# Bias rows in four row tiles, and the output gate's constants moved from POOL to PE for four of six quads

## What is computed

```
x = x + triangle_attention(_gn(x))        # 4 heads of 32, one softmax row of 96 per (i, q, head)
x = x + triangle_multiplication(_gn(x))
```

```
a = mask * sigmoid(zn @ a_g_w.T + a_g_b) * (zn @ a_p_w.T + a_p_b)
b = mask * sigmoid(zn @ b_g_w.T + b_g_b) * (zn @ b_p_w.T + b_p_b)
t = einsum('ikh,jkh->ijh', a, b)
gate = sigmoid(zn @ g_w.T + g_b)
out = gate * (layernorm(t; ln_out_w, ln_out_b) @ z_w.T + z_b)
```

## Time and profile before

| | us |
|---|---|
| runs | 279.98, 281.68, 281.94 |
| median | 281.68 |
| profiled execution, its own time | 281.32 |
| span of its profile | 279.4 |
| busy: PE, DVE, ACT, POOL | 237.3, 210.9, 208.3, 144.1 |

### The profile page before, as it was taken

The page is one execution under the profiler, slowest core; times in us unless marked ns, Lnnn a source line. Parts: engine busy times, 40 slices in busy tenths (PEclk is TensorE's granted clock), DMA queues, the critical chain, the costliest instruction groups (busy, mean ns, idle before and its releaser), DMA issues.

```text
span 279.4 us, 7233 instructions
## 1 busy us (share of the span) xinstructions
PE 237.3 (85%) x2580; PEld 195.4 (70%) x2580; DVE 210.9 (75%) x368; ACT 208.3 (75%) x953; POOL 144.1 (52%) x132
## 2 busy tenths in 40 slices
PE   7569793769999989999999999999979999587930
PEld 7459530757788878788877878888758866386930
DVE  4025892437999989999999989998755849959790
ACT  0374744369999989999999999999846755569490
POOL 1620000008777667777677777675600029998082
PEclk9957959598999999999999999999999999965695
DMA  9300013653444464436453554440000000000028
GB/s 153 50 3 2 1 28 102 205 191 132 159 167 166 167 216 159 159 134 207 164 202 116 174 175 167 149 147 2 2 2 0 0 2 4 0 4 0 0 42 129
DMA packets 42455, 27.12 MB, mean 97 GB/s; under 512 B 24468, under 2 KB 42420, under 8 KB 42420
## 3 DMA queue, kind: packets, MB, share of 16 engines
q1 hardware_dynamic: 31564, 25.22, 27.6%
q10 hardware_dynamic: 10856, 1.45, 3.3%
HBM read 1.36 MB, written 1.18 MB: 9 GB/s over the span
## 4 chain that ended last, share of the span: by engine, by line
PE 41%; ACT 17%; DVE 13%; SPq 8%; issue 7%; ACTq 5%; DMA 5%; POOL 2%; POOLq 1%; DVEq 0%
ACT maps L667 11%; PE psum L1197 5%; SPq L434 5%; DMA u_st<-u_split 5%; PE psum L1074 4%; PE psum L1161 3%; PE psum L1006 3%; PE psum L1208 3%; PE psum L1164 2%; PE psum L1162 2%; PE psum L1139 2%; PE psum L1096 2%; PE psum L1267 2%; DVE shared L987 2%; SPq L413 2%
## 5 line engine op out<-in xcount | busy, mean ns | idle before, releaser
L667 ACT ACTIVATE maps<-psum,neg_max 96x96 f32<-96x96 f32 x384 | 123.6, 353 | 7.8 <-DVE neg_max L925 5.8
L493 POOL TENSOR_TENSOR maps<-maps,rden 96x768 f32<-96x768 f32 x48 | 70.4, 1467 | 79.2 <-DVE rden L935 72.8
L667 ACT ACTIVATION_READ_ACCUMULATOR maps<-psum,neg_max 96x1 f32 x384 | 83.9, 220 | 0.0
L941 DVE COPY turned<-psum 96x1024 f32<-96x1024 f32 x48 | 58.5, 1219 | 8.0 <-PE psum L1197 7.9
L925 DVE TENSOR_REDUCE neg_max<-psum 96x8 f32<-96x768 f32 x48 | 45.8, 954 | 8.8 <-PE psum L1164 8.5
L1197 PE MATMUL psum<-ident,maps 96*96 96x96 f32 x384 | 40.1, 247 | 0.0
L1161 PE MATMUL psum<-u_st,x_stack 128*96 128x384 f32 x96 | 36.6, 382 | 3.3 <-ACT maps L667 2.2
L1162 PE MATMUL psum<-bias_hi,ident_r 128*96 128x384 f32 x96 | 32.8, 341 | 0.0
L1164 PE MATMUL psum<-bias_lo,ident_r 128*96 128x384 f32 x96 | 32.7, 341 | 0.0
L1197 PEld LDWEIGHTS psum<-ident,maps 96*96 96x96 f32 x384 | 32.1, 126 | 0.0
L1208 PE MATMUL psum<-turned 128*32 128x96 f32 x768 | 25.8, 252 | 0.8 <-DVE turned L941 0.8
(11 more groups left out here) (179 smaller groups left out, 423.7 us busy)
## 6 DMA issues: line engine op xcount, KB each, us to landing
u_st<-u_split SPq DMA_DIRECT2D x96, 192.0 KB
x_stack<-shared SPq DMA_DIRECT2D x40, 96.0 KB, 2.0
maps<-in_x ACTq DMA_DIRECT2D x4, 144.0 KB, 4.6
maps<-in_x SPq DMA_DIRECT2D x4, 144.0 KB, 4.0
x_stack<-shared SPq DMA_DIRECT2D x4, 144.0 KB, 2.1
out_y<-maps SPq DMA_DIRECT2D x6, 96.0 KB, 3.1
out_y<-maps ACTq DMA_DIRECT2D x6, 96.0 KB, 3.4
bias_lo<-gate_sb SPq DMA_DIRECT2D x24, 12.0 KB
```

Source lines behind the costliest of these rows:

```text
L493: pool.tensor_tensor(at, at, rden[:, rows, :].unsqueeze(3).to_broadcast([N, 2, H, N]), ALU.mult).then_inc(probs_ready, 1)
L667: e = act.activation(probs[:, k % SLOTS, n, h], bank_s[r % 4][0:N, h * N:(h + 1) * N], ACT.Exp, bias=neg_max[:, r % BODY, h:h + 1], accum_ ...
L941: dve.tensor_copy(turned[0:N, j % 2].rearrange("p r x -> p (r x)"), psum[0:N, 2 * BANK:4 * BANK]).then_inc(t_ready, 1)
```

## The change

**Bias rows.** Rows 0 and 1 of `tri_b` are copied by three DMAs of SP's queue to rows 32, 64 and 96 (and the ones of `ones_r` are set there by three more memsets of DVE at the start). The bias matmul of member f then uses the 32 partitions of f alone.

**Constants.** For quads 2 to 5, gate * constant is no longer added to the residual by POOL. The gate of these quads is multiplied by 1/root before it meets the product, so PE puts constant * root into the bank first and adds the product to it: gate/root * (root * constant + z) = gate * (constant + z/root). For that the root `tok[:, 2]` (now stored in the order of blocks) is transposed by PE, copied by ACT to `deviation_t`, and multiplied by PE with `const_rows`, 96 partitions x 1024, in which POOL has spread `z_const` over the blocks with a 0/1 matrix `selected`. POOL adds gate * constant for the first 8 blocks alone (3 steps in place of 8).

The new tiles lie in memory that attention has left by then, and the reciprocal root is read in the order of blocks:

```
-        gate_const = u_split[0:N, 0:2].bitcast(f32).rearrange("j s t n -> j s (t n)")[:, :, 0:GROUP * HD].rearrange(
-            "j s (b f c) -> j s b f c", f=GROUP, c=C)
+        late = u_split.bitcast(f32).rearrange("p s t n -> p (s t n)")[0:N]
+        const_rows = late[:, 0:2 * 4 * HD].rearrange("p (e x) -> p e x", e=2)
+        deviation_t = late[:, 2 * 4 * HD:2 * 4 * HD + N]
+        selected = late[:, 2 * 4 * HD + N:2 * 4 * HD + N + C]
+        gate_const = late[:, 3 * GN:5 * GN].rearrange("j (s b f c) -> j s b f c", s=2, f=GROUP, c=C)
...
+        CONST_SETS = -(-4 * POOL_QUADS // TRIO)
...
-        inverse = tok[:, 3].rearrange("j b f -> j (b f)").rearrange("j (f b) -> j b f", f=GROUP)
+        inverse = tok[:, 3]
```

SP, behind the last `stage(g)`; PE waits for it before the last idle products of attention (`pe.wait_ge(rows_copied, 16 * (GROUP - 1))`):

```
+            sp.wait_ge(rows_split, 1)
+            for f in range(1, GROUP):
+                sp.dma_start(tri_b[f * C:f * C + 2, :].bitcast(f32), tri_b[0:2, :].bitcast(f32)).then_inc(rows_copied, 16)
```

POOL, behind its last `step_pool`:

```
             pool.wait_ge(z_prep_copied, 1)
-            for n in range(SETS):
-                product = gate_const[:, n % 2, 0:TRIO]
+            pool.wait_ge(selection_made, 1)
+            pool.tensor_tensor(const_rows.rearrange("p e (m c) -> p (e m) c", c=C),
+                               selected.unsqueeze(2).to_broadcast([N, C, C]),
+                               z_const[:, None, 0:C].to_broadcast([N, C, C]), ALU.mult).then_inc(const_spread, 1)
+            for n in range(CONST_SETS):
+                at = slice(TRIO * n, min(TRIO * n + TRIO, 4 * POOL_QUADS))
+                blocks = at.stop - at.start
+                product = gate_const[:, n % 2, 0:blocks]
                 pool.wait_ge(gates_ready, 2 * n + 2)
...
```

ACT, behind the six copies of the tail:

```
             act.wait_ge(var_ready, 5)
-            act.activation(tok[:, 2], tok[:, 1], ACT.Sqrt).then_inc(root_ready, 1)
+            act.activation(tok[:, 2], tok[:, 1].rearrange("j b f -> j (b f)").rearrange("j (f b) -> j b f", f=GROUP),
+                           ACT.Sqrt).then_inc(root_ready, 1)
+            act.wait_ge(deviation_turned, 1)
+            act.activation(deviation_t, banks[0][0:N, 0:N], ACT.Copy).then_inc(deviation_copied, 1)
```

DVE, at its start, at the end of `z_preparation`, and behind `gate_z(1)`:

```
+            for f in range(1, GROUP):
+                dve.memset(ones_r[f * C:f * C + 2, :].bitcast(f32), 1.0)
...
+                dve.tensor_reduce(selected, ident[0:N, 0:N].rearrange("p (g m) -> p m g", m=C), AX.X,
+                                  ALU.add).then_inc(selection_made, 1)
...
-            dve.wait_ge(const_gated, 2 * QUADS)
```

PE, in `project(n)` (the bias matmul of `z_const` in `norm_front(1)` is cut to 32 partitions in the same way):

```
                 for f in range(GROUP):
-                    pe.matmul(projection_bank(n, f)[0:N, 0:TRIO * PW], ones_r[:, :],
-                              tri_b[:, None, 0:PW].to_broadcast([P, TRIO, PW]), start=True, stop=False)
+                    rows = slice(f * C, (f + 1) * C)
+                    pe.matmul(projection_bank(n, f)[0:N, 0:TRIO * PW], ones_r[rows, :],
+                              tri_b[rows, None, 0:PW].to_broadcast([C, TRIO, PW]), start=True, stop=False)
```

PE, in the tail, where the six quads' transposes now stand in a loop of their own ahead of this:

```
+            def z_constant(q):
+
+                rows = slice(32 * (q // 2), 32 * (q // 2) + 32)
+                pe.matmul(z_bank(q)[0:N, :], deviation_t[rows, :], const_rows[rows, q % 2, :], start=True, stop=False)
...
+            z_products(0)
+            pe.wait_ge(tn_ready, QUADS)
+            pe.wait_ge(root_ready, 5)
+            pe.transpose(banks[0][0:N, 0:N], tok[:, 2].rearrange("j b f -> j (b f)"), ident[0:N, 0:N]).then_inc(deviation_turned, 1)
+            z_products(1)
+            pe.wait_ge(deviation_copied, 1)
+            pe.wait_ge(const_spread, 1)
+            for n in range(2):
+                for q in range(POOL_QUADS + n, QUADS, 2):
+                    z_constant(q)
+            for q in range(POOL_QUADS, QUADS):
+                z_products(q)
```

More of the change, by code:

```diff
@@ L336, in res_bank @@
             return 4 + q % RES_BANKS
-        Z_AFTER = 5
         W_ALL = 3 * HD + H + 6 + C
@@ L508, in _ @@
             pool.wait_ge(z_prep_copied, 1)
-            for n in range(SETS):
-                product = gate_const[:, n % 2, 0:TRIO]
+            pool.wait_ge(selection_made, 1)
[6 more added lines that the diff above has]
+                product = gate_const[:, n % 2, 0:blocks]
                 pool.wait_ge(gates_ready, 2 * n + 2)
-                constant = z_const.rearrange("j (f c) -> j f c", f=GROUP)[:, None, :, :].to_broadcast([N, TRIO, GROUP, C])
-                pool.tensor_tensor(product, gate_sb[:, trio(n)], constant, ALU.mult).then_inc(const_gated, 1)
+                constant = z_const.rearrange("j (f c) -> j f c", f=GROUP)[:, None, :, :].to_broadcast([N, blocks, GROUP, C])
+                pool.tensor_tensor(product, gate_sb[:, at], constant, ALU.mult).then_inc(const_gated, 1)
                 pool.wait_ge(const_gated, 2 * n + 1)
-                pool.tensor_tensor(res[:, trio(n)], res[:, trio(n)], product, ALU.add).then_inc(const_gated, 1)
+                pool.tensor_tensor(res[:, at], res[:, at], product, ALU.add).then_inc(const_gated, 1)
                 pool.wait_ge(const_gated, 2 * n + 2)
@@ L1271, in _, with z_products @@
             pe.wait_ge(tri_copied, TRI_BANKS)
-            for q in range(QUADS + Z_AFTER):
-                if q < QUADS:
-                    need(pe, tn_ready, q - 3)
-                    for n in range(4):
-                        mm = pe.transpose(banks[q % 4][:, n * N:(n + 1) * N],
-                                          tri_t[:, 4 * q + n].rearrange("p c f -> p (c f)"), ident[0:N, 0:N])
-                    mm.then_inc(block_t, 1)
-                z = q - Z_AFTER
-                if z >= 0:
-                    pe.wait_ge(tn_ready, z + 1)
-                    for n in range(4):
-                        mm = pe.matmul(z_bank(z)[0:N, n * HD:(n + 1) * HD], tn_t[:, 4 * z + n, :], z_centered,
-                                       start=True, stop=True)
-                    mm.then_inc(z_done, 1)
+            def z_products(q):
+                pe.wait_ge(tn_ready, q + 1)
+                for n in range(4):
+                    mm = pe.matmul(z_bank(q)[0:N, n * HD:(n + 1) * HD], tn_t[:, 4 * q + n, :], z_centered,
+                                   start=q < POOL_QUADS, stop=q < POOL_QUADS or n == 3)
+                mm.then_inc(z_done, 1)
+            def z_constant(q):
+                rows = slice(32 * (q // 2), 32 * (q // 2) + 32)
+                pe.matmul(z_bank(q)[0:N, :], deviation_t[rows, :], const_rows[rows, q % 2, :], start=True, stop=False)
+            for q in range(QUADS):
+                need(pe, tn_ready, q - 3)
+                for n in range(4):
+                    mm = pe.transpose(banks[q % 4][:, n * N:(n + 1) * N],
+                                      tri_t[:, 4 * q + n].rearrange("p c f -> p (c f)"), ident[0:N, 0:N])
+                mm.then_inc(block_t, 1)
+            z_products(0)
[10 more added lines that the diff above has]
+                z_products(q)
 _INS = ["x", "L0_conv_mask", "L0_conv_ln_gamma", "L0_conv_ln_beta", "L0_conv_w_bias", "L0_conv_wq",
```

10 lines of the change are left out of this document (8 added, 2 removed).

## The result

| | us |
|---|---|
| before, beside it | 281.81 (279.98 to 282.27, 4 runs) |
| changed | 278.23 (278.10 to 278.82, 4 runs) |
| ratio | 0.9898, interval 0.9861 to 0.9935 |
| profiled execution of the changed kernel | 278.82, span 277.2 |

Three later comparisons of the same kernel gave 0.9875 [0.9844, 0.9907], 0.9914 [0.9885, 0.9944] and 0.9889 [0.985, 0.9928], so by the medians of each comparison 2.4 to 3.6 us are gained (the two medians above differ by 3.58, a quotient of 0.9873, inside the interval). 281.9 was forecast.

A forecast was written before the change was run, and what follows sets the result against it. Bound: the chain moving between engines in the last 75 us, with DVE and the PE-ACT-DVE bank loop close in the projections. -2.5 + 1.6 + 1.1 = +0.2 on 281.32, median 0.36 higher, so 281.9 us; range 280.3 to 283.6, all cases 279.2 to 284.4.

The forecast's parts named there:

- Parts 1 and 2: Projections: bias rows in four row tiles and POOL's constants for three trios instead of eight; together 2.5 us gained.
- POOL's share: Projections: the first four DVE products each still wait for POOL's whole instruction, 1.01 us; the other four don't.
- The bound of 3.3: Projections: gain of parts 1 and 2 if DVE wins each race against POOL, 3.3 us.
- PE's part: Projections: PE's biases and products per trio fall from 2.1 to 1.4 us, with biases at 0.35 instead of 1.05.
- Part 3: Second layer norm's root: POOL's spreading of `z_const` holds DVE's `tensor_scalar` until it ends; +1.6 us.
- 217.88 plus a handover: Second layer norm: POOL's spreading starts at 218.0, 0.14 after ACT's copy, ahead of DVE's `tensor_scalar` at 218.27.
- rival A: Second layer norm: DVE's `tensor_scalar` doesn't wait for POOL, so only part 4 costs; 280.3 us, chance 0.27.
- B: Tail: the constants fit in PE's slack, so only the `tensor_scalar`'s wait stays; 280.8 us, chance 0.12 as 0.11.
- D: Projections and tail: the row tiles don't overlap; 285.1 us, chance 0.05.
- C: Second transposes: PE's clock falls ahead of them after a 2.0 us pause, +3.1 into the projections; 285.0 us, chance 0.12.
- Part 4: Tail: PE's added transpose and constants make DVE wait 1.0 us for quad 2; +1.1 us (0 to 2.5).
- The wait for quad 2: Tail: DVE wants quad 2 at 4.65 us after quad 0's start, PE delivers at 5.6; wait 1.0 us.

The follow-up runs named there:

- e10: The kernel before, with POOL's gate times constant held back until all sigmoids are done; 288.99 us, one run, its tail of no use.
- e6: The changed kernel with only the bias matmul of `z_const` back on all 128 partitions and the copied rows without its 32 columns; 280.45 us.
- e2: The changed kernel with all bias matmuls, copies and memsets as before, so only the constants moved; 282.71 us.
- e3: The changed kernel with one more POOL product of 96 x 1024 ahead of the spreading, let go by PE's `z_const` matmul; 279.49 us.
- e11: e6 with POOL's spreading of `z_const` let go behind DVE's `tensor_scalar`; 278.29 us.
- e7: The kernel before with the bias rows alone, plus idle PE products ahead of, inside and behind the triangle stage and between the tail's transposes; 277.25 us.
- e13: The changed kernel with PE's constants issued two quads at a time, idle products behind the triangle loop and between the tail's transposes; 276.71 us.

## Why the prediction was wrong

**Parts 1 and 2, forecast -2.5, measured -4.15.** The mechanism was right, the size off, and of two terms. Up to the first mask 0.77 was forecast and 0.65 measured. From there to the triangle product 19.41 was to become about 17.65 (225.5 to 243.15), and became 15.91.

One is POOL's share. The first four products were each to wait for POOL's whole instruction, about 1 us. In the changed kernel two of the eight are longer at all, 1.14 and 1.30, 0.56 us together. e1, in which POOL has all eight constants and only the bias rows are new, shows it too: 16.31 us, with six of eight products at 0.94 to 0.96 (the others take 1.14 and 1.59). By the starts, DVE's product now often comes 0.03 to 0.16 us ahead of POOL's instruction, and then POOL waits: 1.66 us for what takes 1.0. Why DVE's place in that race is the better one when its masks no longer wait for PE is read from the starts, and no run forced the order.

The bound of 3.3 stood for this case ("if DVE wins each race") and entered only as the low end of the range. By it, POOL's share is worth 0.8 us (3.3 against 2.5), and the 4.15 measured lie another 0.85 beyond it. So POOL's share alone doesn't explain the miss; what remains is left for PE's part. How the two divide, no run measures.

The other is PE's part, put at 1.4 us a trio: from the start of the biases to the mask it takes 1.35 now (226.62 to 227.97) against 2.18 in e10 (232.73 to 234.91), so 0.83 less where 0.7 was forecast, and in a dense series 1.01 against 2.05.

That is more than the shared time of the biases gives, by which a trio was to take 0.35 + 1.05: a dense trio takes 1.01, and the idle time of 0.36 us ahead of the products' weight loads (e10) is gone. The Trainium skill says in "TensorEngine Tiling (Array Packing)", section "Key Properties", that a change of the tiling mode drains the engine; the trace agrees in that these gaps go once biases and products use the same four tiles. No run here separates the drain from the overlap of neighbouring trios, which the shared tiles allow too.

**Part 3, forecast +1.6, measured 0.** The failed step is "217.88 plus a handover" against the start of L820. It took ACT's copy at its old place. But the change cuts the bias matmul just ahead of it to 32 partitions, between matmuls of 128, and by e6 the copy comes 0.31 us later for it (216.67 against 216.98): the spreading starts 0.02 us behind the `tensor_scalar` instead of 0.30 ahead. The edit was named and costed nowhere. The mechanism itself, that POOL's instruction holds this one-input instruction whole, is shown by e2, e3 and e6 (1.68, 1.59 and 1.68 us against 0.21). So rival A's outcome came, and not by its reason: that POOL came too late to hold the `tensor_scalar` was luck, by 0.02 us. The Trainium skill's "SBUF — State Buffer", section "SBUF: two separate sides", puts VectorE instructions in a two-port mode or with two SBUF inputs under the exclusive lock of the shared ports. The trace agrees for this `tensor_scalar` of one input (0.21 us alone, 1.68 held), though no row tells its mode; the reciprocal of the same 96 columns, 0.75 us with POOL at work, wasn't held.

**The rivals.** A gave 280.3 and had the part of the `tensor_scalar` right. B had the constants fit in PE's slack, and DVE's wait for quad 2 was there in all four profiles of the changed kernel. D is out by the 0.32 us of the biases. C, at 0.12, didn't come in the changed kernel and came in e6, behind a pause of 1.9 us; in e2 the same pause left the clock at 1.0. Its price was put at 3.1, and it was 1.39: the clock was back at about 224, ahead of the projections.

**Part 4, forecast +1.1, measured +2.48 in the first profile, +1.18 to +1.26 in three others.** The wait for quad 2 was forecast at 1.0 and is 1.52 in the first and 1.17, 1.17 and 1.10 in the others. The constants took 1.96 us (2.0 forecast). So in three of four profiles this term was about right. What was missed is the race of the first profile: later by the wait, DVE's sums meet POOL's sums for quads 0 and 1 in another order. DVE's four sums take 4.33 us together there, against 3.29 in the kernel before and 3.47 in the third profile. A smaller part: +0.37 until the first gate in the first profile, +0.38 in the fourth, and -0.64 and -0.51 in the second and third, with the time at which the clock rises: its mean over 257 to 263 was 0.75 in the first, 0.72 in the fourth, 0.99 in the second and 0.84 in the third profile.

**Sum.** -4.15 + 0.16 + 0.37 + 2.48 + 0.17 = -0.97 from the first mean on, and -1.22 ahead of it by chance of the two executions: together -2.2 us of span. Over its four profiles the changed kernel's mean to end is 69.7 against 72.1, so -2.3; the times say -2.4 to -3.6. Up to 1.3 us of the difference between the two isn't assigned to a stage. Some 0.2 us of it lies outside the span: an execution's own time is longer than its span by 1.83 to 1.88 us on average in the kernel before and by 1.61 to 1.66 in the later comparisons of the changed one. With 1.61 in e1 and 1.83 in e2 it goes with the bias rows; why, no run shows. Against the forecast of +0.2, parts 1 and 2 account for -1.65 and part 3 for -1.6; the tail was +2.1 above its forecast in the first profile and between -0.2 and +0.8 in the others (all stages behind the start of the triangle product, against before).

## What to carry to other kernels

A wait for a shared resource that rests on a start 0.3 us ahead of another must be priced with every edit upstream of that start; let the long instruction go by a semaphore of the one it would hold, as e11 does, and it is no race at all. Take each half of a change by itself: here one half carried the gain, and the other paid only after the wait behind it (the clock of the tail) had gone, and by the profiles alone (0.80 us), not by the times. When an engine stops being late, ask which race for a shared port it now wins, and who pays.

## What the runs showed of the hardware beside that

- A POOL product of 96 x 1024 floats takes 1.91 us alone and holds a DVE `tensor_scalar` of 96 columns (0.21 alone) until its end (1.68 in e2 and e6, 1.59 in e3); it didn't hold a reciprocal of 96 columns (0.75 in both cases).
- The triangle matmuls take 4.20 us for 24 at a granted clock of 1.0 (e7) and 4.22 at 0.5 (the changed kernel, 0.50 over 240 to 245); the transposes and output products of the tail take 4.03 us to the first gate at 1.0 (e7, e13) and 5.84 at the lower one (the changed kernel, first profile).
- In e6 the granted clock was 1.0 from 218 to 220, 0.71 in the two us in which PE came out of a pause of 1.90 us, and 0.50 in the two behind them, in which PE was busy all the time; then 0.94. In the changed kernel, without that pause, it was 1.0 in the same stretch, but so it was in e2 with a pause of 1.89 us.
